# Attended values on quarters of the array, and new written orders for the last stage

## The reference

```
kh = concatenate([kh, bias_k]);  vh = concatenate([vh, bias_v])
weights = softmax(einsum('bqhk,bthk->bhqt', qh, kh) / sqrt(128))
ctx = einsum('bhqt,bthk->bqhk', weights, vh)        # the attended values
x = x + ctx @ wo + bo
```

## Time and profile before

| | |
|---|---|
| median of the runs | 2377.77 us |
| the profiled execution's own time | 2378.71 us |
| its span, first to last instruction | 2376.1 us |
| mean granted clock of TensorE | 0.967 |
| TensorE busy | 2221.2 us, 93% |
| TensorE weight loads | 1763.4 us, 74% |
| VectorE busy | 1237.2 us, 52% |
| ScalarE busy | 948.1 us, 40% |
| GpSimd busy | 317.3 us, 13% |

### The profile page before, as it was taken

The page is one execution under the profiler, slowest core; times in us unless marked ns, Lnnn a source line. Parts: engine busy times, 40 slices in busy tenths (PEclk is TensorE's granted clock), DMA queues, the critical chain, the costliest instruction groups (busy, mean ns, idle before and its releaser), DMA issues. The chain is left out here.

```text
span 2376.1 us, 41148 instructions
## 1 busy us (share of the span) xinstructions
PE 2221.2 (93%) x15874; PEld 1763.4 (74%) x15874; DVE 1237.2 (52%) x2696; ACT 948.1 (40%) x2585; POOL 317.3 (13%) x626
## 2 busy tenths in 40 slices
PE   7899999999979999999999899999999979879975
PEld 6788888788866777777777577777777766656754
DVE  7867767576633333333333233333333317797786
ACT  3344444545523333333333233333333334444442
POOL 2111111010100000000000000000000014332330
PEclk9899999999989999999999999999999989889987
DMA  6000000020005000000000300000000010000000
GB/s 238 9 24 16 22 25 20 16 99 10 10 26 215 14 10 4 13 13 13 13 0 5 80 14 0 13 13 13 13 0 13 5 32 1 10 10 6 9 1 14
DMA packets 60087, 62.96 MB, mean 26 GB/s; under 512 B 16000, under 2 KB 57024, under 8 KB 58304
## 3 DMA queue, kind: packets, MB, share of 16 engines
q1 hardware_dynamic: 59968, 61.29, 7.9%
HBM read 50.79 MB, written 10.49 MB: 26 GB/s over the span
## 5 line engine op out<-in xcount | busy, mean ns | idle before, releaser
L1421 ACT ACTIVATE l2a_exps<-l2a_ps_s,l2a_shift 128x65 f32<-128x65 f32 x512 | 154.4, 314 | 299.6 <-DVE l2a_shift L1481 299.6
L1410 ACT ACTIVATE l2a_qT<-l2a_ps_q,cols 128x256 f32<-128x256 f32 x256 | 107.5, 471 | 393.0 <-PE l2a_ps_q L1555 393.0
L1607 PE MATMUL l2a_ps_y<-shared,l2a_oT 128*128 128x256 f32 x1024 | 242.4, 380 | 1.1 <-ACT l2a_oT L1427 1.1
L1469 DVE TENSOR_SCALAR l2a_kT<-l2a_ps_k,cols 128x256 f32<-128x256 f32 x256 | 112.1, 479 | 194.8 <-PE l2a_ps_k L1555 193.7
L1607 PEld LDWEIGHTS l2a_ps_y<-shared,l2a_oT 128*128 128x128 f32 x1024 | 184.6, 190 | 21.3 <-ACT l2a_oT L1427 1.5
L1495 DVE COPY l2a_pT<-l2a_ps_p 64x256 f32<-64x256 f32 x256 | 107.9, 421 | 122.4 <-PE l2a_ps_p L1586 120.7
L1477 DVE TENSOR_REDUCE l2a_row_max<-l2a_ps_s 128x4 f32<-128x260 f32 x128 | 54.9, 429 | 191.7 <-PE l2a_ps_s L1578 191.7
L1596 PE MATMUL l2a_ps_o<-l2a_pT,l2a_v 128*128 128x128 f32 x1024 | 148.1, 288 | 0.0
L1384 POOL TENSOR_TENSOR l2a_learned<-l2a_exps,l2a_inv_sum 128x4 f32<-128x4 f32 x128 | 26.1, 204 | 871.9 <-DVE l2a_probs L1488 871.9
L1596 PEld LDWEIGHTS l2a_ps_o<-l2a_pT,l2a_v 128*128 128x128 f32 x1024 | 124.0, 191 | 8.8
L1555 PEld LDWEIGHTS l2a_ps_k<-l2a_cT,shared 128*128 128x128 f32 x512 | 97.9, 191 | 38.3 <-issue 27.8
(11 more groups left out here) (265 smaller groups left out, 4366.9 us busy)
## 6 DMA issues: line engine op xcount, KB each, us to landing
f_c_tile<-in_ctx SPq DMA_DIRECT2D x16, 256.0 KB, 4.1
between<-f_final SPq DMA_DIRECT2D x16, 256.0 KB, 2.1
l2a_c_tile<-in_ctx SPq DMA_DIRECT2D x16, 256.0 KB, 2.7
shared<-in_l_wo SPq DMA_DIRECT2D x2, 2048.0 KB, 17.9
inside<-l2a_y_out SPq DMA_DIRECT2D x16, 256.0 KB, 2.2
f_x_tile<-in_x SPq DMA_DIRECT2D x8, 256.0 KB, 5.4
shared<-in_l_w SPq DMA_DIRECT2D x2, 1024.0 KB, 10.7
l_mlp_w<-in_l_mlp_w SPq DMA_DIRECT2D x2, 1024.0 KB, 10.9
```

The lines of the kernel that those rows point to most:

```text
L1410: last = nc.scalar.activation(qT[:, n, :], ps_q[:, n * ROUND:(n + 1) * ROUND], ACT.Identity, bias=col(f"l2_bq{a + 1}", 2 * p + n), scale=1.0)
L1421: nc.scalar.activation(exps[:, m, :], ps_s[:, m * KEYS:(m + 1) * KEYS], ACT.Exp, bias=shift[:, m:m + 1], scale=scale, accum_out=row_sum[:, ...
L1469: last = nc.vector.tensor_scalar(kT[:, n, :, 0:SEQ], ps_k[:, n * ROUND:(n + 1) * ROUND].rearrange("d (m k) -> d m k", k=SEQ), col(f"l2_bk{ ...
L1607: nc.tensor.matmul(ps_y[:, u * DIM:(u + 1) * DIM], oT[:, n, u].rearrange("d b q -> d (b q)"), wo[:, 2 * p + n, :], start=(p == 0 and n == ...
```

## The change

In the wide attention, `pT` loses its block-diagonal form and with it the zeros. Each product of `attend` is cut in four: the keys of one sequence (64 rows), one half of the head's features (64 columns), and the 64 queries of the same sequence. These are four quarters of the array. The results of the sequence `u = 0` go to `ps_o`, those of `u = 1` to the second half of `ps_p`. TensorE's `transpose_probs` now waits until ScalarE has copied the attended values of the pair before. `attended_out` copies one sequence at a time instead of one head at a time, and the learned weights are transposed into `ps_x`. In the last stage the lists of the four engines TensorE, VectorE, ScalarE and GpSimd are replaced by others with the same steps; SyncE's list stays.

```diff
--- before.py
+++ after.py
@@ -1264,13 +1264,14 @@
         inv_sum = sb("inv_sum", [P, 2 * NU])
         learned = sb("learned", [P, NU, P])
         learnedT = sb("learnedT", [P, NU, P])
-        pT = sb("pT", [P, 2 * NB, NU, SEQ])
+        pT = sb("pT", [P, 2 * NB, SEQ])
         oT = sb("oT", [P, 2, NU, NB, SEQ])
         res_b = sb("res_b", [P, 2, DIM])
         y_out = sb("y_out", [P, 2, DIM])
         value_gap = sb("value_gap", [P, HEADS, ONES + 1])
         gap_out = sb("gap_out", [P, DIM])
         ps_q, ps_k, ps_v, ps_s, ps_p, ps_o, ps_y, ps_x = (bank(n) for n in "qkvspoyx")
+        o_half = [ps_o[:, 0:ROUND], ps_p[:, ROUND:2 * ROUND]]
         norm = Normed(nc, sb, sem, x_tile, ps_x, lambda c: col(f"l2_ln{a}_s", c), lambda c: col(f"l2_ln{a}_b", c), ident)
         hT = norm.hT
 
@@ -1365,10 +1366,9 @@
             nc.gpsimd.memset(value_gap[:], 0.0).then_inc(set_up, 1)
             nc.gpsimd.memset(gap_out[:], 0.0).then_inc(set_up, 1)
             nc.gpsimd.memset(learned[:], 0.0).then_inc(set_up, 1)
-            nc.gpsimd.memset(pT[:], 0.0).then_inc(set_up, 1)
+            pool.wait_ge(set_up, 5)
+            nc.gpsimd.memset(learned[:, :, ONES:ONES + 1], 1.0).then_inc(set_up, 1)
             pool.wait_ge(set_up, 6)
-            nc.gpsimd.memset(learned[:, :, ONES:ONES + 1], 1.0).then_inc(set_up, 1)
-            pool.wait_ge(set_up, 7)
             norm.inverse_deviations(pool, 0)
 
             def learned_key(i, p):
@@ -1423,14 +1423,14 @@
 
             def attended_out(i, p):
                 act.wait_ge(o_in_psum, per_pair(i, p))
-                for n in range(2):
-                    last = nc.scalar.activation(oT[:, n], ps_o[:, n * ROUND:(n + 1) * ROUND].rearrange("d (b u q) -> d u b q", b=NB, u=NU),
+                for u in range(NU):
+                    last = nc.scalar.activation(oT[:, :, u].rearrange("d n b q -> d n (b q)"), o_half[u].rearrange("d (n t) -> d n t", n=2),
                                                 ACT.Copy)
                 last.then_inc(o_ready, 1)
 
             def learned_transposed(i):
                 act.wait_ge(learnedT_in_psum, count(i, 1, 0))
-                nc.scalar.activation(learnedT[:].rearrange("h u q -> h (u q)"), ps_p[:, ROUND:2 * ROUND], ACT.Copy
+                nc.scalar.activation(learnedT[:].rearrange("h u q -> h (u q)"), ps_x[:, 0:ROUND], ACT.Copy
                                      ).then_inc(learnedT_ready, 1)
 
             def slot(i, j, made, attended, projected, more):
@@ -1492,7 +1492,7 @@
                 dve.wait_ge(pT_in_psum, per_pair(i, p))
                 for u in range(NU):
                     half = slice(u * SEQ, (u + 1) * SEQ)
-                    last = nc.vector.tensor_copy(pT[half, :, u, :], ps_p[half, 0:ROUND].rearrange("k (m q) -> k m q", q=SEQ))
+                    last = nc.vector.tensor_copy(pT[half], ps_p[half, 0:ROUND].rearrange("k (m q) -> k m q", q=SEQ))
                 last.then_inc(pT_ready, 1)
 
             def add_residual(i):
@@ -1521,7 +1521,7 @@
                 if j == 3 and more:
                     norm.normalised(dve, i + 1)
                 if j == -1:
-                    dve.wait_ge(set_up, 7)
+                    dve.wait_ge(set_up, 6)
                     dve.wait_ge(folded_in_psum, 1)
                     nc.vector.tensor_copy(gap_out[0:ONES + 1, :], ps_y[0:ONES + 1, 0:DIM]).then_inc(folded_ready, 1)
                     dve.wait_ge(folded_ready, 1)
@@ -1582,20 +1582,29 @@
 
             def transpose_probs(i, p):
                 pe.wait_ge(p_ready, per_pair(i, p))
+                if p:
+                    pe.wait_ge(o_ready, per_pair(i, p - 1))
+                elif not isinstance(i, int) or i:
+                    pe.wait_ge(o_ready, per_pair(i - 1, PAIR - 1))
                 for n in range(2):
                     last = nc.tensor.transpose(ps_p[:, n * P:(n + 1) * P], probs[:, n * NU:(n + 1) * NU, :].rearrange("q u k -> q (u k)"), ident)
                 last.then_inc(pT_in_psum, 1)
 
             def attend(i, p):
                 g, first = divmod(2 * p, 4)
+                pe.wait_ge(set_up, 6)
                 pe.wait_ge(pT_ready, per_pair(i, p))
                 if first == 0:
                     pe.wait_ge(v_ready, value_event(i, g, 1))
                 for n in range(2):
                     for b in range(NB):
-                        last = nc.tensor.matmul(ps_o[:, n * ROUND + b * P:n * ROUND + (b + 1) * P],
-                                                v[g % 2][b][:, (first + n) * WIDE:(first + n + 1) * WIDE],
-                                                pT[:, n * NB + b].rearrange("k u q -> k (u q)"), start=True, stop=True)
+                        at = n * NB + b
+                        for u in range(NU):
+                            keys_of = slice(u * SEQ, (u + 1) * SEQ)
+                            for dims in (slice(0, WIDE // 2), slice(WIDE // 2, WIDE)):
+                                d = (first + n) * WIDE + dims.start
+                                last = nc.tensor.matmul(o_half[u][dims, at * SEQ:(at + 1) * SEQ], v[g % 2][b][keys_of, d:d + WIDE // 2],
+                                                        pT[keys_of, at], start=True, stop=True)
                 last.then_inc(o_in_psum, 1)
 
             def project_out(i, p):
@@ -1610,7 +1619,7 @@
             def learned_value(i):
                 pe.wait_ge(learned_ready, per_pair(i, PAIR - 1))
                 for u in range(2):
-                    last = nc.tensor.transpose(ps_p[:, ROUND + u * P:ROUND + (u + 1) * P], learned[:, u, :], ident)
+                    last = nc.tensor.transpose(ps_x[:, u * P:(u + 1) * P], learned[:, u, :], ident)
                 last.then_inc(learnedT_in_psum, 1)
 
             def add_learned_value(i):
...
 TAIL_TENSOR_ORDER = """
-xm:0 u0:0 u1:0 d0:0 d1:0 u2:0 u3:0 d2:0 xm:1 d3:0 u0:1 u1:1 d0:1 d1:1 x1:0 u2:1 u3:1 lo:0 d2:1 mx:0 d3:1 xm:2 m4:0
-u0:2 kp:0 rp:0 x1:1 u1:2 vp:0 gp:0 dc:0 sp1:0 rt:0 lo:1 d0:2 sp0:0 ru:0 d1:2 u2:2 u3:2 d2:2 mx:1 d3:2 os0:0 os1:0 rp:1
-me:0 vp:1 va:0 kp:1 dc:1 x1:2 rt:1 sp1:1 m4:1 lo:2 ru:1 yp:0 sp0:1 gp:1 mx:2 os0:1 os1:1 rp:2 me:1 m4:2 x2:0 kp:2 va:1
...
+xm:0 u2:0 u0:0 u1:0 u3:0 d0:0 d1:0 d2:0 d3:0 xm:1 u2:1 u3:1 u0:1 x1:0 u1:1 d0:1 lo:0 d1:1 mx:0 d2:1 d3:1 vp:0 kp:0
+dc:0 sp0:0 rp:0 m4:0 rt:0 sp1:0 x1:1 gp:0 ru:0 xm:2 u2:2 u1:2 u0:2 os0:0 u3:2 d0:2 d1:2 d2:2 os1:0 d3:2 me:0 lo:1 va:0
+mx:1 m4:1 kp:1 x1:2 rp:1 yp:0 vp:1 gp:1 sp0:1 dc:1 x2:0 rt:1 lo:2 ru:1 fk:0 sp1:1 xm:3 m4:2 u0:3 u2:3 gp:2 u3:3 u1:3
+mx:2 os0:1 fr:0 os1:1 rp:2 fv:0 me:1 vp:2 kp:2 dc:2 sp0:2 va:1 d0:3 sp1:2 d1:3 d2:3 d3:3 rt:2 yp:1 ru:2 x1:3 x2:1 fk:1
+fr:1 xm:4 fv:1 u2:4 u3:4 os0:2 u0:4 u1:4 os1:2 d0:4 me:2 lo:3 va:2 mx:3 d1:4 d2:4 d3:4 rp:3 yp:2 dc:3 kp:3 vp:3 x2:2
+sp0:3 rt:3 m4:3 x1:4 fr:2 fk:2 sp1:3 fv:2 gp:3 ru:3 xm:5 u2:5 u0:5 u1:5 d0:5 d1:5 d2:5 os0:3 os1:3 u3:5 me:3 lo:4 va:3
+mx:4 d3:5 rp:4 yp:3 dc:4 kp:4 vp:4 x2:3 sp0:4 rt:4 x1:5 m4:4 fr:3 fk:3 sp1:4 fv:3 gp:4 ru:4 xm:6 u2:6 u3:6 u0:6 u1:6
+d0:6 d1:6 os0:4 os1:4 d2:6 me:4 lo:5 va:4 mx:5 d3:6 rp:5 yp:4 vp:5 kp:5 dc:5 sp0:5 x2:4 rt:5 m4:5 x1:6 fr:4 fk:4 sp1:5
+fv:4 gp:5 xm:7 ru:5 u2:7 u0:7 u1:7 os0:5 u3:7 d0:7 d1:7 d2:7 os1:5 d3:7 me:5 lo:6 va:5 mx:6 m4:6 kp:6 x1:7 rp:6 yp:5
+vp:6 gp:6 sp0:6 dc:6 x2:5 lo:7 rt:6 mx:7 fk:5 fr:5 kp:7 fv:5 vp:7 m4:7 rp:7 sp0:7 gp:7 dc:7 sp1:6 rt:7 sp1:7 ru:6
+os0:6 ru:7 os1:6 me:6 os0:7 va:6 os1:7 me:7 yp:6 va:7 x2:6 yp:7 fr:6 fk:6 x2:7 fv:6 fk:7 fr:7 fv:7
 """
 TAIL_VECTOR_ORDER = """
-ma:0 ma:1 ma:2 mo:0 la:0 sm:0 p0:0 p2:0 mo:1 p1:0 la:1 rk:0 sm:1 ga:0 a10:0 a11:0 a12:0 a13:0 sc11:0 a00:0 a01:0
-sc10:0 a02:0 a03:0 sc00:0 sc01:0 rm00:0 rm01:0 ow:0 rm10:0 p0:1 p2:1 oo:0 p1:1 mo:2 ce:0 la:2 rc:0 nm:0 rk:1 sm:2
-a10:1 a11:1 gd:0 a12:1 a13:1 sc11:1 a00:1 r2:0 a01:1 sc10:1 a02:1 a03:1 sc00:1 sc01:1 rm00:1 rm01:1 ow:1 rm10:1 na:0
...
+ma:0 ma:1 ma:2 mo:0 la:0 sm:0 p0:0 p2:0 p1:0 mo:1 la:1 a00:0 a01:0 a02:0 a03:0 rk:0 a10:0 a11:0 a12:0 sc01:0 ga:0 ow:0
+sc00:0 rm00:0 rm01:0 a13:0 sc11:0 sc10:0 rm10:0 sm:1 oo:0 mo:2 ce:0 la:2 p0:1 rc:0 nm:0 p2:1 p1:1 gd:0 sm:2 rk:1 r2:0
+na:0 ga:1 a00:1 ma:3 a01:1 a02:1 s2:0 a03:1 sc01:1 a10:1 rm01:1 a11:1 a12:1 a13:1 sc11:1 sc00:1 rm00:1 ow:1 sc10:1
+rm10:1 p0:2 p2:2 oo:1 ga:2 p1:2 o1:0 o2:0 ce:1 rk:2 a00:2 a01:2 a02:2 a03:2 rc:1 a10:2 nm:1 a11:2 a12:2 gd:1 a13:2
+mo:3 la:3 r2:1 na:1 sc01:2 rm01:2 ma:4 s2:1 ow:2 sc11:2 sc00:2 rm00:2 o1:1 o2:1 sc10:2 rm10:2 sm:3 oo:2 ce:2 p0:3 rc:2
+nm:2 p2:3 p1:3 gd:2 mo:4 la:4 r2:2 na:2 rk:3 ma:5 s2:2 a00:3 a01:3 a02:3 a03:3 sc00:3 rm00:3 a10:3 a11:3 a12:3 a13:3
+o1:2 o2:2 ga:3 ow:3 sc10:3 sc11:3 sc01:3 rm01:3 rm10:3 sm:4 oo:3 ce:3 p0:4 rc:3 nm:3 p2:4 p1:4 gd:3 mo:5 la:5 r2:3
+na:3 rk:4 ma:6 s2:3 a00:4 a01:4 a02:4 a03:4 sc00:4 rm00:4 a10:4 a11:4 a12:4 a13:4 o1:3 o2:3 ga:4 sc11:4 sc01:4 rm01:4
+sc10:4 ow:4 rm10:4 sm:5 oo:4 ce:4 p0:5 rc:4 nm:4 p2:5 p1:5 gd:4 mo:6 la:6 r2:4 na:4 rk:5 ma:7 a00:5 s2:4 a01:5 a02:5
+a03:5 sc01:5 a10:5 rm01:5 a11:5 a12:5 o1:4 o2:4 ga:5 sc00:5 rm00:5 ow:5 a13:5 sc11:5 sc10:5 rm10:5 sm:6 oo:5 mo:7 ce:5
```

(6 more changed lines are left out.)

47 lines of the change are left out of this document (13 added, 34 removed).

## The result

The changed kernel took 2340.31 us, the median of four runs (2336.5 to 2343.07), against 2377.59 us before in the same comparison (2370.87 to 2378.65): a ratio of 0.9849, with a 95% interval from 0.983 to 0.9867. The gain is 37.3 us where 45.8 had been forecast (32.3 and 13.5); the time lies in the range and in the forecast's own range. Nearly all of it comes from the attention. The last stage gave less than a third of its term.

A forecast was written before the change was run, and what follows sets the result against it. TensorE's stream was taken to bound the middle stage, the interlock of TensorE and VectorE the last. From 2378.7, minus 32.3 and 13.5, came 2332.9; the median, 0.9 lower, gave 2332 us, range 2306 to 2358 (8 in 10).

The forecast's parts named there:

- the forecast's own range: Whole kernel: 2320 to 2345 us, the case in which no rival holds, given 57%.
- The attended values: Wide attention, `attend`: four quarters side by side, 0.74 us against 1.00 a pair, over 128 pairs 32 us gained.
- The choice between L1097 and L959: `attend`: row groups changing every four MATMULs overlap fully as in L1097; partly as in L959, it would take 1.2 us.
- The rival of starts no closer than 0.029 us: `attend`: spacing limits all starts, 1.19 us against 1.00, a loss of 25 us, kernel at 2389 us; chance 9%.
- The side costs put at zero: Beside `attend`: new wait before `transpose_probs` (at most 0.4 us in two pairs a call), copies, `pT` zeroing, learned transposes: zero.
- The orders: Last stage, new lists with one MLP in each job: 321 us against 337.5 from job 0 to 7, gain 13.5 us.
- the turn of 49.5 us: Last stage, one job on VectorE: 40.6 us of work, 8.2 of waiting, 0.7 between instructions; four such intervals, 198 us.
- the 65 us of the interval behind it: Last stage, job 5 to job 6: 40.6, 18 and 6.5 us, as job 7's steps stand before job 6's `rm10`.
- the walk's waits: Last stage, VectorE per job: 1.9 us for `me`, 4.0 after `ce`, 2.3 for `r2`, `rk` and `s2`; 8.2 in all.
- No step's length changes: Last stage: the new lists leave every step's length as it was; only who is late changes.
- Behind job 7: Last stage's end: 40.5 us before, plus 3 us for leftover work of job 6.
- The clock: Last stage: TensorE's granted clock above 0.93, with no 20 us at 0.6, as a sign of the forecast.

The follow-up runs named there:

- the two halves alone: Two kernels, against the kernel before: the changed attention with the old lists, 2345.32 us (0.9875); the old attention with the new lists, 2371.78 us (0.9985).

## Why the prediction was right or wrong

**The attended values: mechanism right, size right to 2 us.** `attend` and the exposed load came to 0.727 us of the forecast 0.743, so a pair gained 0.268 instead of 0.252. That alone would have made the term larger than 32.3. It came out smaller, 30.6 by the rounds and 29.8 in the kernel with this part alone, because the two calls' last rounds ended no earlier (59.50 us both times). Six of their seven pairs did gain; one `attend` in each was waited out, the wait for the softmax grew from 1.65 to 2.11 us, and behind it the clock fell, which cost 1.6 us. The prediction had looked at those pairs for the new wait alone. It had put nothing for what a longer wait does to the clock, though its rows for the last stage had shown the clock low where TensorE waits.

**The choice between L1097 and L959 was right, and now has a cause.** The same MATMULs in two orders show that the row groups' alternation decides: after four, 0.625 us; after 16, 0.906. The second number lies on the side of L959, where 16 in a row overlapped only in part.

**The rival of starts no closer than 0.029 us is refuted:** 32 MATMULs start within 0.48 us, 0.015 apart on average. So is the rule that the Trainium skill's page TensorE: Matmul & The Clock Gate (The mechanism) states, of matmuls in strict order, as far as row groups go: in the order with the sequence outermost the second row group starts while six MATMULs of the first are still to come. A line of its own for each row group, of limited length, would give all the starts shown here; that limit was not measured.

**The side costs put at zero were zero.** TensorE waits at the transposes (L1590) for VectorE's probabilities, in a call's last round, and not for L1427. The 0.4 us at L1616 for L1427 was 0.53 before. Another engine became the bound at that one place only, where it had been the bound before.

**The orders: 13.5 us was mis-sized; about 3.9 was measured.** The step that failed is the turn of 49.5 us, "8.2 us of waiting and 0.7 between instructions on 40.6 of work", and the 65 us of the interval behind it. Neither half of it held. Over the six intervals up to job 6 VectorE's work was 273.6 us for 261.6, and waits and gaps were 59.8 for 48.4; the one turn that met the walk's waits (9.05 us against 8.2) was a good one, and the turn of job 5 had 13.6 us of waits and gaps.

The work grew because the prediction took its mean from a trace in which some of it was held by GpSimd, and assumed that "No step's length changes". VectorE's instructions with both inputs in SBUF run longer while GpSimd works. Counted from one start to the next, the scan takes 0.583 us free and up to 2.71 beside it, L2212 in the median 0.609 and 1.258, L2219 0.691 and 1.163; those that read one input from a PSUM bank do not (L2129 0.395 and 0.392, L2162 0.591 and 0.593). Worked out as the length above each line's free median, summed over the stage, it is some 35 us before and 44 in the change (likewise in the two halves alone): the new lists put 9 us more of the one beside the other. In the change the mixes hold for some 22 us and `rm11` for 16.4; of the 9 us that were added, `rm11` has 5, the mixes and the residual L1883 two or three each. The Trainium skill's page SBUF — State Buffer (Who interferes with whom) has a rule for this, that a VectorE instruction with two SBUF inputs contends with a GpSimd instruction that reads SBUF and one with a single SBUF input, outside the modes that use two ports, does not. The lines above agree on both counts.

That this holding exists and lengthens VectorE's work is shown by the cuts. That it is the gain which the lists lack is not. Taking away `rm11` took 5 us of the 9 and did not set the lists further apart. With the mixes cut too, their difference grew from about 4 to about 10 us, and with the mixes went both a holding of VectorE and a wait of TensorE, 10.1 us, that only the new lists have and that the prediction had nothing for. So some 6 of the 9.6 us missing hang on the mixes, by one way or the other. What is left, some 3 us, stays open; the holding by L1883, which no run cut, is 4 us with the new lists and 1 to 2 with the old, and would be of that size.

**The intervals.** From job 5 to job 6 it was 75.1 us and not 65, of which 5.6 more is VectorE's work and 4.5 its waits and gaps. The start of the stage was 5.3 us shorter, where nothing had been put. Behind job 7 it was 36.7 us where 43.5 had been put: the prediction took 40.5 from the first half of job 7's step, while its other end, job 0 at 1998.09, is a second half; from the second half it was 38.8 before. These errors hid most of the shortfall in the middle (22 us), so the total looked nearer than its parts. That the last stage gained at all is, measured against this walk, partly luck.

**The clock.** Above 0.93, with no 20 us at 0.6, was wrong. The stage's mean is 0.91 after 0.90, and the stretch in which TensorE starves keeps its low clock:

```profile
2280.00:2300.00 20.00, 6.86 (x39) 3.24 (x40) 18.93 (x26) 1.91 (x2) 3.24 (x1) 0.58 0.00 0
2300.00:2320.00 20.00, 12.24 (x46) 8.70 (x45) 13.64 (x23) 7.11 (x12) 1.30 (x4) 0.67 0.00 0
```

VectorE is busy for 18.93 of 20 us there: the new lists moved the starving to the end and did not remove it. Between them and the stage's first 20 us (0.66) no 20 us fell below 0.83.

## What to carry to other kernels

Splitting a product over quarters pays when the load's columns set its step and when the row groups alternate at short distance; the same instructions written one row group after the other gave all of it back. Count a saving per iteration only where the engine is the bound, and look at the granted clock behind each wait that the saving makes longer: in the last rounds here it took back what six pairs had earned. Check a walk against every turn and not against one. A mean duration taken from a trace belongs to the neighbours it had: before an order is planned from step lengths, split VectorE's SBUF-only steps into those with and those without GpSimd beside them. The total of a group can stay, as the scans' did, while steps that were free in the old order are held in the new one.

## What the runs showed of the hardware

- Where the load has 64 columns, a float32 MATMUL costs 0.058 us of its part of the array, with 17, 64 or 65 columns moving. With a load of 128 columns and 64 moving it costs 0.11, as with 128 moving.
- A MATMUL of one row group started ahead of six written before it for another row group.
- Behind a wait of 2.11 us TensorE's granted clock fell to its lower level in 17 of 20 cases, and eight MATMULs of 256 columns took up to 3.3 us instead of 1.9. Behind a wait of 1.65 us, in the four cases of the old attention, it did not fall.
- A scan of 256 elements on 128 partitions, 0.583 us alone, took up to 2.71 us beside GpSimd. Moving eight products of 128 by 1024 from GpSimd to VectorE made VectorE's busy time 6 us smaller.
